# GpSimd makes the lower left area of a triangular inverse, step by step beside VectorE

## The reference

```
G = Kc.T @ Kc + 1e-4 * I          # 64 x 64
W = solve(G, Kc.T @ Vc)
U = I[:, :8]
for _ in range(2): U, _ = qr(W @ U)
Wr = U @ (U.T @ W)
S = 0.9 * S + Wr
out = 0.125 * (Qc @ S)
```

## Time and profile before

| | |
|---|---|
| device time, median of 3 runs | 1578.5 us (1574.62 to 1580.41) |
| the profiled execution | 1578.29 us, of which its span (first to last instruction) 1576.5 us |
| mean granted TensorE clock | 0.811 of full speed |
| busy: VectorE / TensorE / ScalarE / GpSimd | 1293.8 / 994.5 / 650.0 / 225.0 us |
| products L1553 and additions L1561 | 608 instructions each, 308.9 and 303.7 us |

### The profile page before, as it was taken

The page is one execution under the profiler, slowest core; times in us unless marked ns, Lnnn a source line. Parts: engine busy times, 40 slices in busy tenths (PEclk is TensorE's granted clock), DMA queues, the critical chain, the costliest instruction groups (busy, mean ns, idle before and its releaser), DMA issues.

```text
span 1576.5 us, 48154 instructions
## 1 busy us (share of the span) xinstructions
PE 994.5 (63%) x19646; PEld 792.3 (50%) x19646; DVE 1293.8 (82%) x3840; ACT 650.0 (41%) x1366; POOL 225.0 (14%) x149
## 2 busy tenths in 40 slices
PE   1344910596276789777789876773474832997165
PEld 1333510464265667666667665662463721776144
DVE  5884589859998779899779799889489789889677
ACT  3563610264143456543456543452242520664032
POOL 3551001101102001302001302001500000001200
PEclk9555965698589899988889988897687975999577
DMA  2555100011000001110001110012220200210000
GB/s 73 174 174 181 30 25 0 2 29 41 1 4 3 4 10 44 39 59 4 4 6 47 32 53 3 4 37 81 66 72 1 72 16 0 78 31 24 9 14 23
DMA packets 52109, 61.94 MB, mean 39 GB/s; under 512 B 4048, under 2 KB 32416, under 8 KB 51888
## 3 DMA queue, kind: packets, MB, share of 16 engines
q1 hardware_dynamic: 51888, 58.84, 12.1%
HBM read 38.31 MB, written 20.51 MB: 37 GB/s over the span
## 4 chain that ended last, share of the span: by engine, by line
PE 46%; DVE 26%; issue 10%; ACT 5%; POOL 2%; DMA 1%; POOLq 0%; SPq 0%; DVEq 0%; ACTq 0%
PE a_bank L688 6%; DVE a_blocks L1561 5%; DVE a_outer L1553 5%; PE a_bank L826 5%; PE a_bank L759 4%; PE a_bank L933 4%; PE a_bank L816 3%; PE a_bank L832 3%; PE a_bank L702 3%; PE a_bank L914 3%; PE a_bank L948 3%; PE a_bank L884 2%; PE a_bank L777 2%; PE a_bank L787 2%; ACT a_work L1076 1%
## 5 line engine op out<-in xcount | busy, mean ns | idle before, releaser
L1553 DVE TENSOR_TENSOR a_outer<-a_blocks 128x512 f32<-128x512 f32 (+19 forms) x608 | 308.9, 541 | 11.7
L1561 DVE TENSOR_TENSOR a_blocks<-a_blocks,a_outer 128x512 f32<-128x512 f32 (+19 forms) x608 | 303.7, 532 | 0.8
L1076 ACT ACTIVATE a_work<-a_bank 128x512 f32<-128x512 f32 (+1 forms) x193 | 110.3, 602 | 215.7 <-PE a_bank L798 174.3
L1466 POOL TENSOR_TENSOR a_root<-a_recip,a_half 128x32 f32<-128x32 f32 (+2 forms) x24 | 91.6, 3819 | 699.0 <-DVEq L1576 692.2
L798 PE MATMUL a_bank<-a_ident,a_blocks 128*128 128x128 f32 x256 | 36.5, 311 | 167.2 <-DVE a_blocks L1612 165.6
L1076 ACT ACTIVATE a_solve<-a_bank 128x512 f32<-128x512 f32 (+2 forms) x184 | 87.9, 523 | 108.1 <-PE a_bank L832 50.2
L688 PE MATMUL a_bank<-a_wk,a_cg 128*128 128x512 f32 x256 | 121.2, 619 | 0.0
L798 PEld LDWEIGHTS a_bank<-a_ident,a_blocks 128*128 128x128 f32 x256 | 35.4, 201 | 167.9 <-DVE a_blocks L1612 125.9
L1076 ACT ACTIVATE a_xb<-a_bank 128x512 f32<-128x512 f32 x112 | 63.5, 597 | 90.6 <-PE a_bank L933 54.1
L1076 ACT ACTIVATE a_scaled<-a_bank 128x512 f32<-128x512 f32 (+1 forms) x130 | 65.4, 530 | 78.0 <-PE a_bank L816 68.1
L816 PE MATMUL a_bank<-a_solve,a_work 32*32 32x64 f32 x4096 | 58.2, 247 | 62.3 <-issue 49.0
(11 more groups left out here) (197 smaller groups left out, 2236.1 us busy)
## 6 DMA issues: line engine op xcount, KB each, us to landing
f_x<-in_L_attn_x SPq DMA_DIRECT2D x16, 256.0 KB, 3.1
s_xnt<-f_xt SPq DMA_DIRECT2D x16, 256.0 KB, 2.1
s_c<-f_cm SPq DMA_DIRECT2D x16, 256.0 KB, 2.3
s_base<-f_base SPq DMA_DIRECT2D x16, 256.0 KB, 2.8
a_cg<-s_c SPq DMA_DIRECT2D x16, 256.0 KB, 2.8
a_cc<-s_c SPq DMA_DIRECT2D x16, 256.0 KB, 3.9
a_xnt<-s_xnt SPq DMA_DIRECT2D x16, 256.0 KB, 3.9
a_base_in<-s_base SPq DMA_DIRECT2D x13, 256.0 KB, 2.6
```

Source lines behind the costliest of these rows:

```text
L1076: nc.scalar.activation(out, view, ACT.Copy, scale=scale).then_inc(emptied, 1)
L1466: nc.gpsimd.tensor_tensor(root[:, :, a:b], recip[:, :, a:b], half[:, :, a:b], ALU.pow).then_inc(roots_ok, 1)
L1553: return ch.inc(V.tensor_tensor(product, bcast(column, 2, area.shape[2]), bcast(row, 3, area.shape[3]), ALU.mult))
L1561: return ch.inc(V.tensor_tensor(area, area, product, ALU.add))
```

## The change

In steps 1 to 15 of each factorisation the left product and the left addition (2 x 15 instructions) leave VectorE and go to GpSimd, which replaces `roots` by `left(block_, n)`: for each j it waits until the step's column is there, multiplies, waits for itself, adds, and waits for itself again. After the fifteenth it goes on with the three `pow` instructions as before. The columns are announced by a new semaphore `columns_ok` (3 counts per step, 47 per factorisation), and the left results by `left_ok` (30 per factorisation). VectorE waits for `left_ok` once per factorisation, at step 16, between its near and its left product. Steps 16 to 31 keep their left area on VectorE.

The order on VectorE changes as well. In steps j < 15 it becomes: clear the diagonal, scale two parts, near product, right product, clear, near addition, next reciprocal, right addition. In steps above 15 it becomes: scale, clear the diagonal, near product, left product, clear, near addition, next reciprocal, left addition. The count of VectorE's chain (`LINKS`) is now taken from the emitted instructions.

The core of the diff (the helper `strip` moves out of `factor` unchanged, so that both engines can call it):

```diff
-                def roots(n):
-
+                def left(block_, n):
+
+                    m, ops = by_columns(block_), 0
+                    for j in range(1, KEPT):
+                        area, column, row, product = strip(m, j, "left")
+                        pool.wait_ge(columns_ok, n * COLUMNS + (min(3 * j + 3, COLUMNS) - COLUMNS))
+                        nc.gpsimd.tensor_tensor(product, bcast(column, 2, area.shape[2]), bcast(row, 3, area.shape[3]), ALU.mult).then_inc(left_ok, 1)
+                        pool.wait_ge(left_ok, n * LEFTS + (ops + 1 - LEFTS))
+                        nc.gpsimd.tensor_tensor(area, area, product, ALU.add).then_inc(left_ok, 1)
+                        ops += 2
+                        pool.wait_ge(left_ok, n * LEFTS + (ops - LEFTS))
+                    assert ops == LEFTS
                     for i, (a, b) in enumerate(ROOTS):
...
-                roots(1)
-                roots(2)
+                left(lead_blocks, 1)
+                left(schur_blocks, 2)
                 with pool.Fori(0, G - 1) as g:
-                    roots(g * 2 + 3)
+                    left(lead_blocks, g * 2 + 3)
                     lengths(g)
-                    roots(g * 2 + 4)
+                    left(schur_blocks, g * 2 + 4)
                     combine(g)
...
                         if j + 1 < HB:
-                            if j + 1 < end:
-                                column = negated(m[:, :, j, j + 1:end], m[:, :, j, j + 1:end], j)
                             if j < KEPT:
-                                column = negated(m[:, :, j, KEPT:HB], m[:, :, KEPT:HB, j], j)
-                            cleared = ch.inc(V.memset(m[:, :, j, j], 0.0))
-                            ch.wait(cleared)
-                            if j < KEPT:
+                                V.memset(m[:, :, j, j], 0.0).then_inc(columns_ok, 1)
+                                if j + 1 < KEPT:
+                                    negated(m[:, :, j, j + 1:KEPT], m[:, :, j, j + 1:KEPT], j).then_inc(columns_ok, 1)
+                                negated(m[:, :, j, KEPT:HB], m[:, :, KEPT:HB, j], j).then_inc(columns_ok, 1)
+                                columns_made(j)
                                 near = multiply(j, "near")
-                                left = multiply(j, "left")
-                                settled = add(j, "near", near)
                                 right = multiply(j, "right")
                             else:
-                                left = multiply(j, "left")
-                                near = multiply(j, "near")
+                                ch.inc(negated(m[:, :, j, j + 1:HB], m[:, :, j, j + 1:HB], j))
+                                ch.link(V.memset(m[:, :, j, j], 0.0))
+                                multiply(j, "near")
+                                if j == KEPT:
+                                    dve.wait_ge(left_ok, n * LEFTS)
+                                near = left = multiply(j, "left")
                         if j:
                             ch.inc(V.memset(m[:, :, j:HB, j - 1], 0.0))
                         if j + 1 < KEPT:
+                            settled = add(j, "near", near)
                             inverse = pivot(j + 1, settled)
-                            add(j, "left", left)
                             add(j, "right", right)
                         elif j + 1 == KEPT:
                             settled = add(j, "right", right)
-                            add(j, "left", left)
                             inverse = pivot(j + 1, settled)
                         elif j + 1 < HB:
                             settled = add(j, "near", near)
+                            inverse = pivot(j + 1, settled)
                             add(j, "left", left)
-                            inverse = pivot(j + 1, settled)
```

More of the change, by code:

```diff
@@ L61 @@
 KEPT = 16
-FACTOR_LINKS = 9 * HB + 6
+COLUMNS = 3 * KEPT - 1
+LEFTS = 2 * (KEPT - 1)
 ROOTS = ((0, 16), (16, 28), (28, HB))
@@ L600, in main_pass @@
         pivots_ok, roots_ok = sem("pivots_ok"), sem("roots_ok")
+        columns_ok, left_ok = sem("columns_ok"), sem("left_ok")
         schur_in, schur_out = sem("schur_in"), sem("schur_out")
@@ L651, in rows, with strip @@
             return slice(s * DH, s * DH + DH) if half is None else slice(s * DH + half * HB, s * DH + half * HB + HB)
+        def strip(m, j, which):
+            if j < KEPT:
+                i, c = {"near": ((j + 1, KEPT), (0, HB)), "left": ((KEPT, HB), (0, j)), "right": ((KEPT, HB), (KEPT, HB))}[which]
+            else:
+                i, c = {"near": ((j + 1, HB), (KEPT, HB)), "left": ((j + 1, HB), (0, KEPT)), "right": ((0, 0), (0, 0))}[which]
+            n_i, n_c = i[1] - i[0], c[1] - c[0]
+            if n_i * n_c == 0:
+                return None
+            at = {"near": 0, "left": 2 * KEPT * HB, "right": 2 * KEPT * (HB + KEPT)}[which]
+            product = outer_all[:, at:at + 2 * n_i * n_c].rearrange("p (s c r) -> p s c r", s=2, r=n_i)
+            return m[:, :, c[0]:c[1], i[0]:i[1]], m[:, :, j, i[0]:i[1]], m[:, :, c[0]:c[1], j], product
         def beside(first, second):
@@ L1338, in main_pass @@
         UNITS += SPARE
-        LINKS = 2 * FACTOR_LINKS + 4 * R + 6 * (R - 1)
         with nc.Block() as block:
@@ L1531, in factor, with columns_made @@
                     diagonal = block_[:, :, 0:HB * HB:HB + 1]
-                    space = {"near": 0, "left": 2 * KEPT * HB, "right": 2 * KEPT * (HB + KEPT)}
-                    def strip(j, which):
-                        low = min(j // KEPT, 1) * KEPT
-                        if j < KEPT:
[L1538 to L1546, removed]
+                    def columns_made(j):
+                        dve.wait_ge(columns_ok, n * COLUMNS + (min(3 * j + 3, COLUMNS) - COLUMNS))
                     def multiply(j, which):
-                        at = strip(j, which)
+                        at = strip(m, j, which)
                         if at is None:
@@ L1567, in negated @@
                     def negated(out, src, j):
-                        return ch.inc(V.scalar_tensor_tensor(out, src, -1.0, bcast(recip[:, :, j], 2, src.shape[2]), ALU.mult, ALU.mult))
+                        return V.scalar_tensor_tensor(out, src, -1.0, bcast(recip[:, :, j], 2, src.shape[2]), ALU.mult, ALU.mult)
                     settled = ch.inc(V.tensor_scalar(diagonal, diagonal, RIDGE_EPS, None, ALU.add))
@@ L1687, in _ @@
                     ch.link(fp4_weights(nc, ch, buf, n, NBF, fp4_tmp))
+                made = ch.n
                 lead(0)
+                made = ch.n - made
                 for buf, at, n in ffn_w[4:]:
@@ L1693, in _ @@
                 first = ch.n
+                LINKS = 2 * made + 4 * R + 6 * (R - 1)
                 with dve.Fori(0, G - 1) as g:
@@ L1698, in _ @@
                     orthogonalise(g)
-                    made = ch.n - first
-                assert made == LINKS
+                    assert ch.n - first == LINKS
                 ch.base, ch.n = (G - 1) * LINKS, first
```

1 line of the change is left out of this document (removed).

## The result

The changed kernel takes 1601.16 us (median of 4 runs, 1597.13 to 1606.31); the kernel before, run beside it, 1576.56 us (4 runs, 1572.55 to 1580.41). The ratio is 1.0158, with a 95% interval of 1.0113 to 1.0203: slower by 24.6 us. The forecast was 1608.0, the range 1588 to 1636. The profiled execution of the changed kernel took 1606.31 us and is the longest of the four; its span is 1604.5 us, 28.0 more than the 1576.5 before. The forecast for the difference was 29.7.

The account below looks back on a forecast made before the run. The ends of F1, F2 and F8, plus F4 to F7 beyond their slack, were taken as the bound. With D = 7.0 us, 14.0 + 8.7 + 7.0 = 29.7 us on 1578.3 gave 1608.0 us, range 1588 to 1636.

Parts of the forecast that it names:

- The bound: TensorE's waits for factorisations: F1, F2 and F8 count fully; F3 to F7 have 2.3 to 10.7 us of slack.
- the prediction's own ladder: Sum of delays over F1 to F8 after each slack: 29.7 us for a growth of 7.0 us per factorisation.
- D: Growth of one factorisation: 15.0 us stall less 8.2 us gain, +6.8 us, taken as +7.0.
- What VectorE gains: Per factorisation, VectorE alone: 10.3 us of left instructions less 2.1 us for the new order, 8.2 us.
- the exposed reciprocals: In steps 0 to 15 the reciprocal directly follows the near addition: 0.13 us each, 16 times, 2.1 us.
- The second half: Steps 16 to 31: the reciprocal is exposed, but the left addition hides it from the next scaling; taken as equal.
- What GpSimd costs: GpSimd's two-input left work stalls VectorE 1.0 us per 512 elements, 15.0 us per factorisation.
- Queues and waits: VectorE's `left_ok` wait at step 16 costs nothing, or 1 us if turns fall badly; left work behind `combine` keeps up.
- The signs named in advance: Profile after: 240 more GpSimd instructions, F2 about 94.6 us, 6 or 7 TensorE waits, VectorE's 512-element additions 1.2 to 1.7 us.
- Overlap: Rival, chance 0.10: left instructions overlap with VectorE as at `pow`; each factorisation 8.2 us shorter, kernel 1554 us.
- Longer or behind: Rival, chance 0.09: GpSimd holds VectorE longer or VectorE waits at step 16; +14.1 us per factorisation, 1661 us.
- Small ones hide: Rival, chance 0.05: most stall of the first seven steps falls into gaps; growth below 2.6 us, 1579 to 1586 us.

Follow-up runs that it names:

- the probe "two": Kernel before plus, in steps 1 to 15, signals and two GpSimd two-input instructions per step on tiles VectorE doesn't use; 1695.92 us.
- the probe of 12 elements: Kernel before plus, in steps 1 to 15, signals and one two-input GpSimd `pow` of 12 elements per step; F1 took 89.88 us.
- the four probes: Kernel before plus signals in steps 1 to 15, with GpSimd instructions none, write-only, one-input or two-input; 1589.95, 1585.57, 1615.13 and 1695.92 us.

## Why the prediction was right

**The bound.** Right. F1, F2 and F8 count with all of their length, F3 keeps its slack, and F4 to F7 pass on what exceeds theirs. Forecast and measured delay at F4 to F7 beyond F2: 0.9 and 2.8, 3.5 and 3.8, 4.0 and 5.3, 8.7 and 8.2 us. The end: 29.7 forecast, 27.3 at the end of F8, 28.0 in the span, and 24.6 between the medians. Put through the prediction's own ladder, the eight measured D give 24.8 us, with 2.2, 3.2, 4.9 and 7.9 at F4 to F7. So the ladder of slacks was right, and the 5 us between forecast and medians are the size of D.

**What VectorE gains.** Right: 8.2 us forecast, 8.7 in F1 and 8.0 in F2. Its parts held too: 10.3 forecast for the 30 instructions and 10.1 and 9.9 measured; 2.1 for the exposed reciprocals, and 1.3 and 1.8 for order and signals together. The second half, costed as equal, took 33.0 us instead of 32.8 in F2.

**What GpSimd costs.** Mechanism right, size 6% too large: 15.0 forecast, 14.1 measured. The difference of each step of F2 between the changed kernel and the one without the left work shows where. Times are from one reciprocal to the next, in us:

| step | before | after | without left work | stall | left elements, both instructions |
|---|---|---|---|---|---|
| 1 | 3.89 | 3.88 | 3.82 | 0.06 | 64 |
| 2 | 3.75 | 3.88 | 3.68 | 0.20 | 128 |
| 5 | 3.54 | 3.85 | 3.27 | 0.58 | 320 |
| 8 | 3.32 | 3.81 | 2.84 | 0.97 | 512 |
| 11 | 3.12 | 3.80 | 2.44 | 1.36 | 704 |
| 14 | 2.99 | 3.84 | 2.13 | 1.71 | 896 |

The stall grows by (1.71 - 0.06)/(896 - 64) = 2.0 ns per element, and 0.06 us per step is hidden. That is GpSimd's own rate as taken from the earlier trace rows. Those rows compare two different operations, but one operation gives the same: in the probe "two", GpSimd's shortest products take 0.26 us for 32 elements and 0.72 for 256, 2.05 ns per element. So while GpSimd streams two inputs, VectorE stands. For one input the stop is 0.71 ns per element and this sentence does not hold. The forecast took 1.0 us per 512 elements, which is 1.95 ns; the 0.9 us too many are about the 0.06 hidden in each of 15 steps. VectorE needs 1.03 ns per element and 0.08 us per instruction for the same work. That is why none of steps 1 to 14 wins more than 0.01 us, and why the loss grows with the step: in the small steps, where the price per instruction could have made GpSimd worthwhile, VectorE pays for the exposed reciprocal. Only step 15 is shorter (3.48 instead of 3.95), since VectorE's own last left addition no longer lies before the reciprocal of pivot 17; step 16 takes 0.32 of that back.

**D.** The forecast of 7.0 was rounded up from 6.8; F1 and F8 measured 5.4, F2 and F3 6.1 and 6.0. Of the 1.4 us between 6.8 and F1, 0.9 is the stall and 0.5 the gain of 8.7.

**What the forecast missed.** In F4 and F6 D is 8.3 and 8.2: 2.1 to 2.2 us of it are the two `combine` instructions, which the ladder didn't have there. This made up for part of the smaller stall: with D = 6.1 in F4 and F6 the ladder would end at 20.9 instead of 24.8 us. So the total came close partly by luck, for two reasons that oppose each other. Also, in the profiles F1 starts 1.4 us later and TensorE needs 0.9 more between F1 and F2, both costed at nothing. These are not the change's: over the runs here F1 starts between 202.2 and 204.5 us (before 202.9, changed 204.3, the changed kernel with `combine` held 202.2), and F1's end and F2's start lie 41.5 to 46.4 us apart (42.9 before, 43.9 changed). So of the 27.3 us at the end of F8, 2.3 are such differences from run to run, and what is left, 25.0, agrees with the medians.

**Queues and waits.** At step 16 VectorE never stood at `left_ok`. GpSimd's last addition ended at 402.94 and VectorE's near product began at 403.04. But the scaling of that step took 0.87 us beside this addition (401.41 to 402.94), and step 16 took 3.17 instead of 2.85 us. These 0.3 us lie between the forecast's "nothing" and "1 us if the turns fall badly". In F5 and F7 the left work behind `combine` kept up, as forecast: their second halves are as long as F3's, 33.1 us.

**The signs named in advance.** The instruction counts, TensorE's 6 waits, F2's length (94.6 forecast, 93.8 measured) and GpSimd's 480-element instructions (1.2 to 1.8 forecast; 1.48 and 1.53) came true. One did not, and here the mechanism was placed wrongly within the step: VectorE's 512-element right additions keep 0.69 us in steps 1 to 14 of F2 (in step 15 it takes 1.41). In these steps the stall sits on the right product and on the near addition (in step 7, where near has 512 elements too, the near product takes 0.69 us, the right one 1.08 and the near addition 1.09), because GpSimd starts at the head of the step and has finished by the right addition. The forecast's own sign of being wrong was "if VectorE's 512-element instructions kept 0.68 us"; these additions kept it, the right products of the same size did not.

**The rivals.** *Overlap*: excluded; what looked like overlap at `pow` is an instruction that is long but reads 32 elements, as the probe of 12 elements shows. *Longer or behind*: excluded here, 1.84 ns per element net (14.1 us over 7,680 elements) and no wait at step 16. *Small ones hide*: true for 0.06 us per step, not more. Its price didn't fit its reason either: the first seven steps hold 28/120 of the elements, 3.5 of the 15.0 us, so hiding all of it would still leave D = 3.3, not under 2.6.

The Trainium skill, SBUF — State Buffer, "SBUF: two separate sides", states that whichever of a two-input VectorE instruction and a GpSimd instruction starts first gets the shared ports for the whole instruction. The runs here disagree: 39.5 us of `pow` with two inputs cost 0.24 us. The statement of the same page in "Who interferes with whom", that a VectorE instruction with two SBUF inputs contends with a GpSimd instruction that reads SBUF and not with one that only writes, agrees with the four probes (0.1 us for writes, 5.3 and 14.9 us for readers).

## What to carry to other kernels

Before giving elementwise work from a busy VectorE to GpSimd, compare what GpSimd's reading costs VectorE with what the work costs VectorE itself: here 2.0 against 1.03 ns per element for two inputs, so every element moved costs twice what it frees (VectorE's 0.08 us per instruction come back besides). By the probes here, what can be given away is work that reads little, however long it lasts, or only writes, and only if its time on VectorE was not already covered by a neighbour. And put the slack of every stage into the sum first: with 2 to 11 us of slack, a D of 5 to 8 us per factorisation became about 25 us over eight of them.

## What the runs showed that was not expected

- **A signal of its own costs VectorE 0.12 to 0.14 us.** The probe with signals alone adds 15 increments per factorisation and takes 2.1 us more in F1 (89.64 against 87.58) and 1.8 in F2 (89.59 against 87.76).
- **One input is a third of two, not half.** 0.71 against 2.02 ns per element, though the one-input instructions kept GpSimd busy longer.
- **A factorisation inside the loop is longer.** The first half of F1 and F8, outside it, took 59.8 and 59.9 us in the changed kernel, that of F2, F4 and F6, inside it, 60.8 (F3, also inside, 60.5). Without the left work it is 46.5 against 47.4, so this has nothing to do with GpSimd's reads; in the kernel before both are 54.9 to 55.0. Only the changed kernel and those made from it let VectorE wait for `columns_ok` at every step, with a count that depends on the loop there and is constant outside. That this is the cause was not tested.
